# A hybrid convolution and state-space block with a ternary FFN on one core: out-projection bias by one-row matmuls, two loads exchanged, and the first FFN step's instruction lists reordered

## What is computed

```
x1 = LN(x)                                  # no weights
u, v = split(x1 @ W_in + b_in)              # 512 -> 2 x 512
v = silu(v); v = conv3(v, conv_w) + conv_b  # depthwise, along the 8192 tokens
h_t = a * h_(t-1) + b * v_t ;  y_t = c * h_t + d * v_t     # a = sigmoid(logit_a)
out = (u * silu(y)) @ W_out + b_out         # b_out is the bias of this change
x = x + LN( LN_weighted(out + x1) )
f = gelu(LN(x) @ ternary(W1).T + b1)        # 512 -> 2048
x = x + LN( f @ ternary(W2).T + b2 )        # 2048 -> 512
```

## Time and profile before

| | |
|---|---|
| median of 3 runs | 1426.45 us (1423.77 to 1429.59) |
| the profiled execution | 1427.28 us |
| its span, first to last instruction | 1425.1 us |
| mean granted TensorE clock | 0.998 |
| TensorE matmul (PE), weight load (PEld) | 98%, 45% of the span |
| VectorE, ScalarE, GpSimd | 79%, 62%, 29% |
| HBM read, written | 31.49 MB, 16.78 MB |

### The profile page before, as it was taken

How to read it: one execution, slowest core, us unless ns; L and a number is a source line. 1 busy time by engine, 2 the same in 40 slices (tenths; PEclk the granted TensorE clock), 3 DMA queues, 4 the chain that set the end, 5 groups by cost and what they waited for, 6 DMA issues and landing times.

```text
span 1425.1 us, 19037 instructions
## 1 busy us (share of the span) xinstructions
PE 1402.7 (98%) x6528; PEld 642.0 (45%) x6528; DVE 1119.9 (79%) x1892; ACT 878.4 (62%) x1263; POOL 418.3 (29%) x518
## 2 busy tenths in 40 slices
PE   7999999999999999999999999999999999999997
PEld 5444444444444444444444444444444444444443
DVE  7999987867878687796867878677796877998734
ACT  7899575646656565665656756466565656753443
POOL 4234151321413233142321413224132321523221
PEclk9999999999999999999999999999999999999999
DMA  9712321311312112111311203123121231001200
GB/s 249 242 43 77 72 71 19 89 30 30 89 19 72 30 45 75 30 60 31 82 37 30 75 15 89 31 30 89 24 66 30 51 69 30 30 1 30 59 31 30
DMA packets 155985, 82.00 MB, mean 58 GB/s; under 512 B 132721, under 2 KB 132721, under 8 KB 155761
## 3 DMA queue, kind: packets, MB, share of 16 engines
q1 hardware_dynamic: 155888, 80.79, 22.2%
HBM read 31.49 MB, written 16.78 MB: 34 GB/s over the span
## 4 chain that ended last, share of the span: by engine, by line
PE 82%; DVE 6%; issue 3%; ACT 1%; POOL 1%; DMA 0%; SPq 0%; DVEq 0%; ACTq 0%; POOLq 0%
PE f2b L580 14%; PE f2b L581 14%; PE f1b L551 13%; PE f1b L552 13%; PE misc L519 6%; PE misc L517 6%; PE misc L518 6%; PE misc L533 3%; PE misc L531 3%; PE misc L532 3%; DVE bn L775 1%; POOL rsc L2009 0%; DVE vl L851 0%; DVE g_lo L895 0%; DVE ring L793 0%
## 5 line engine op out<-in xcount | busy, mean ns | idle before, releaser
L580 PE MATMUL f2b<-w,ring 128*128 128x512 fp8e5 x1008 | 382.2, 379 | 1.2 <-DVE ring L793 1.0
L581 PE MATMUL f2b<-w,ring 128*128 128x512 fp8e5 x1008 | 382.0, 379 | 0.0
L551 PE MATMUL f1b<-x3T,w 128*128 128x512 f16 x960 | 364.0, 379 | 0.6 <-DMA x3T<-tp 0.4
L552 PE MATMUL f1b<-x3T,w 128*128 128x512 f16 x960 | 363.8, 379 | 0.0
L1587 ACT ACTIVATE ring<-f1b,par 128x512 f32<-128x512 f32 x256 | 175.1, 684 | 232.9 <-PE f1b L552 232.6
L2008 POOL TENSOR_SCALAR ve<-mv 128x4 f32<-128x4 f32 (+2 forms) x88 | 35.5, 403 | 731.0 <-DVE mv L785 730.8
L793 DVE SCALAR_TENSOR_TENSOR ring<-ring,f_sc 128x512 f16<-128x512 f32 x256 | 210.1, 835 | 40.8 <-ACT ring L1597 40.6
L1597 ACT ACTIVATE ring<-ring,f_sc 128x512 f16<-128x512 f32 x256 | 180.1, 710 | 0.0
L517 PE MATMUL misc<-x1T,win_hi 128*128 128x512 f16 x456 | 172.9, 379 | 0.0
L518 PE MATMUL misc<-x1T,win_hi 128*128 128x512 f16 x456 | 172.9, 379 | 0.0
L519 PE MATMUL misc<-x1T,win_lo 128*128 128x512 f16 x456 | 172.9, 379 | 0.0
(11 more groups left out here) (219 smaller groups left out, 2017.2 us busy)
## 6 DMA issues: line engine op xcount, KB each, us to landing
out_dram<-hb SPq DMA_DIRECT2D x64, 256.0 KB, 2.0
xs<-x_dram SPq DMA_DIRECT2D x14, 1024.0 KB, 5.6
ring<-w1t_dram SPq DMA_DIRECT2D x3, 1024.0 KB, 12.3
stage<-w2t_dram SPq DMA_DIRECT2D x3, 1024.0 KB, 8.5
x1T<-tp SPq DMA_TRANSPOSE x68, 3.1
...
```

Of the source, the lines that this page charges most:

```text
L551: pe.matmul(b[:, :], w, src[:, k, :], start=k == 0, stop=False)
L552: mm = pe.matmul(b[:, :], w, src[:, KC + k, :], start=False, stop=k == KC - 1)
L580: pe.matmul(f2b[q][:, :], h_hi[:, i % H_SLOTS, qs], w2[:, j, :], start=j == 0, stop=False)
L581: mm = pe.matmul(f2b[q][:, :], h_lo[:, i % H_SLOTS, qs], w2[:, j, :], start=False, stop=j == FC - 1)
```

## The change

1. **Bias.** VectorE's four `add_bias(j)` of tile 0 go. `wo_forward` (VectorE) computes one column o_fwd, the product of both scales; `out_bias` on ScalarE writes b_out times o_fwd into one row of xn (fp32), and `out_bias` on TensorE multiplies a row of ones (1 x 128) with it (1 x 512) into each of the four accumulators of o(0, j) with start=True; the matmuls of o(0, j) then add to them. `h_add(0, j)` waits for x1_hi instead of ob_ok.
2. **Loads.** SP issues the third x tile ahead of W_out.
3. **Warming.** `keep_warm` issues 4 warm matmuls behind each of the first three transposes of tile 0, 12 in place of 30; `ffn_scale` (TensorE) goes from the list's first place to behind it, `setup_params` (VectorE) from the first place to behind x_stats(1, 3).
4. **Lists.** The hand-written lists of all engines up to the end of the first FFN step are put in another order, with new ORDER and SIGNED. Among it: centre_tap(1, 0) and (1, 1) go from ahead of the transposes of x3 to behind the copies of x3; o(1, 1) and o(1, 2) get f2(0, 4) between them, o(1, 2) and o(1, 3) f2(0, 5); in_proj("v", 3, 0) to (3, 3) come ahead of f1(0, 12). The loops of later steps are unchanged.

The diff, cut to its core (VectorE's and ScalarE's lists behind o(0, j) are left out for the most part):

```diff
 
 
 W1_CHUNK, W2_CHUNK = "w1", "w2"
-ORDER = [(W1_CHUNK, 0), (W1_CHUNK, 2), (W1_CHUNK, 3), (W1_CHUNK, 1), (W1_CHUNK, 5), (W1_CHUNK, 6), (W1_CHUNK, 10), (W1_CHUNK, 9),
-         (W2_CHUNK, 0), (W1_CHUNK, 7), (W1_CHUNK, 4), (W1_CHUNK, 8), (W2_CHUNK, 1), (W1_CHUNK, 11), (W2_CHUNK, 2), (W2_CHUNK, 3),
-         (W2_CHUNK, 4), (W2_CHUNK, 7), (W2_CHUNK, 5), (W2_CHUNK, 6), (W2_CHUNK, 8), (W1_CHUNK, 14), (W1_CHUNK, 13), (W1_CHUNK, 15),
-         (W1_CHUNK, 12), (W2_CHUNK, 11), (W2_CHUNK, 9), (W2_CHUNK, 10), (W2_CHUNK, 13), (W2_CHUNK, 12), (W2_CHUNK, 14), (W2_CHUNK, 15)]
-SIGNED = (1, 1, 1, 1, 2, 2, 3, 3, 4, 2, 2, 3, 5, 3, 8, 6, 7, 7, 7, 7, 9, 10, 10, 10, 10, 9, 9, 9, 11, 11, 11, 11)
+ORDER = [(W1_CHUNK, 0), (W1_CHUNK, 3), (W1_CHUNK, 2), (W1_CHUNK, 1), (W1_CHUNK, 6), (W1_CHUNK, 5), (W1_CHUNK, 4), (W1_CHUNK, 7),
+         (W1_CHUNK, 9), (W1_CHUNK, 11), (W1_CHUNK, 8), (W1_CHUNK, 10), (W2_CHUNK, 0), (W2_CHUNK, 1), (W2_CHUNK, 2), (W2_CHUNK, 3),
+         (W2_CHUNK, 4), (W2_CHUNK, 5), (W2_CHUNK, 7), (W2_CHUNK, 9), (W2_CHUNK, 6), (W2_CHUNK, 11), (W2_CHUNK, 10), (W2_CHUNK, 8),
+         (W1_CHUNK, 14), (W1_CHUNK, 15), (W1_CHUNK, 12), (W1_CHUNK, 13), (W2_CHUNK, 12), (W2_CHUNK, 13), (W2_CHUNK, 14), (W2_CHUNK, 15)]
+SIGNED = (1, 1, 1, 1, 2, 2, 2, 2, 3, 3, 3, 3, 4, 5, 6, 7, 8, 8, 8, 9, 8, 9, 9, 9, 10, 10, 10, 10, 11, 11, 11, 11)
 
 
...
             transposes("t1", 1)
+            load_x(2)
             sp.dma_start(wo_raw, w_out_d).then_inc(wout_in, 16)
-            load_x(2)
             load_w1(0)
             load_w1(1)
...
 
-                out_ = take("o", c, j)
+                out_ = take("o", c, j) if c > 0 else bank("o", 0, j)
                 js = slice(j * P, (j + 1) * P)
                 if c == 0 and j == 0:
                     pe.wait_ge(wo_l, KC)
                 for k in range(KC):
                     pe.wait_ge(glo_ok, KC * c + k + 1)
-                    pe.matmul(out_[:, :], g_hi[:, k, js], wo_hi[:, k, :], start=k == 0, stop=False)
+                    pe.matmul(out_[:, :], g_hi[:, k, js], wo_hi[:, k, :], start=c > 0 and k == 0, stop=False)
                     pe.matmul(out_[:, :], g_hi[:, k, js], wo_lo[:, k, :], start=False, stop=False)
                     mm = pe.matmul(out_[:, :], g_lo[:, k, js], wo_hi[:, k, :], start=False, stop=k == KC - 1)
...
             def keep_warm():
 
-                pe.wait_ge(x1_lo, 3)
-                warm(14)
-                for k in (1, 3):
-                    pe.wait_ge(win_l, k)
-                    warm(8)
+                for j in range(NB - 1):
+                    wait_transposed(pe, block_no["t1", 0, j])
+                    warm(4)
 
             def transpose_x3(n):
...
+            def out_bias():
+
+                pe.wait_ge(ob_ok, 2)
+                for j in range(NB):
+                    pe.matmul(take("o", 0, j)[:, :], ones[0:1, :], xn[0:1, :], start=True, stop=False)
+
...
             pe.wait_ge(const_ok, 2)
-            ffn_scale()
             pe.wait_ge(x1_hi, 1)
             warm(6)
             win_sum(1)
             warm(6)
             keep_warm()
+            ffn_scale()
             in_proj("v", 0, 0, v_mm)
             in_proj("v", 0, 1, v_mm)
...
             in_proj("v", 1, 2, v_mm)
-            wo_sum()
             in_proj("v", 1, 3, v_mm)
             in_proj("u", 0, 0, u_mm)
+            wo_sum()
             in_proj("u", 0, 1, u_mm)
             in_proj("u", 0, 2, u_mm)
             in_proj("u", 0, 3, u_mm)
+            out_bias()
             o(0, 0)
             o(0, 1)
             o(0, 2)
...
             f1(0, 5)
             f1(0, 6)
             f1(0, 7)
+            f2(0, 0)
+            f1(0, 8)
             f2(0, 1)
-            f1(0, 8)
+            f1(0, 9)
             f2(0, 2)
-            f1(0, 9)
+            f1(0, 10)
             f2(0, 3)
-            f1(0, 10)
-            f2(0, 4)
             o(1, 0)
             o(1, 1)
+            f2(0, 4)
             o(1, 2)
+            f2(0, 5)
             o(1, 3)
-            f2(0, 5)
+            f2(0, 6)
             f1(0, 11)
-            f2(0, 6)
+            f2(0, 7)
+            in_proj("v", 3, 0, v_mm)
+            f2(0, 8)
+            in_proj("v", 3, 1, v_mm)
+            in_proj("v", 3, 2, v_mm)
+            in_proj("v", 3, 3, v_mm)
+            f2(0, 9)
             f1(0, 12)
-            f2(0, 7)
+            f2(0, 10)
             f1(0, 13)
-            f2(0, 8)
             f1(0, 14)
-            in_proj("v", 3, 0, v_mm)
-            in_proj("v", 3, 1, v_mm)
-            f2(0, 9)
-            in_proj("v", 3, 2, v_mm)
-            f2(0, 10)
+            f2(0, 11)
             f1(0, 15)
-            f2(0, 11)
...
                 else:
-                    ve_.wait_ge(ob_ok, j + 1)
+                    ve_.wait_ge(x1_hi, j + 1)
                     ve_.wait_ge(wo_sc_ok, 2)
                 dst = hb_of(c)[:, j, :]
...
 
+            def wo_forward():
+
+                after("wo inverse")
+                ve_.wait_ge(scale_ok, 3)
+                ve_.tensor_scalar(o_fwd[:, :], wq[:, 5:6], w_mul[:, 0:1], ACT_SCALE / 2.0 ** 14, ALU.mult, ALU.mult).then_inc(ob_ok, 1)
...
@@ -1194,118 +1199,116 @@
             t_lo("t1", 0, 0)
             win_square(1)
             t_lo("t1", 0, 1)
+            x_stats(1, 0)
+            x_stats(1, 1)
             win_total(1)
-            x_stats(1, 0)
+            aggr(0, 1, 0)
             win_power(1)
-            x_stats(1, 1)
+            aggr(0, 1, 1)
             win_bound(1)
-            aggr(0, 1, 0)
-            aggr(0, 1, 1)
+            t_lo("t1", 0, 2)
             win_scale(1)
-            t_lo("t1", 0, 2)
             x_stats(1, 2)
             t_lo("t1", 0, 3)
+            aggr(0, 1, 2)
             x_stats(1, 3)
-            aggr(0, 1, 2)
+            setup_params()
+            aggr(0, 1, 3)
             setup_split(0)
-            aggr(0, 1, 3)
             setup_split(1)
             setup_split(2)
             setup_split(3)
+            v_scale()
+            ffn_total()
             t_lo("t1", 1, 0)
-            v_scale()
             t_lo("t1", 1, 1)
             win_max_u(0)
             t_lo("t1", 1, 2)
             win_max_u(1)
+            ffn_exponent()
+            win_square(0)
             t_lo("t1", 1, 3)
-            win_square(0)
-            taps(0, 0, True)
             win_total(0)
             win_power(0)
             win_bound(0)
             win_scale(0)
-            ffn_total()
+            ffn_inverse()
+            taps(0, 0, True)
+            setup_split(KC + 0)
             taps(0, 1, True)
-            setup_split(KC + 0)
             setup_split(KC + 1)
-            ffn_exponent()
-            ffn_inverse()
             ffn_scale()
             setup_split(KC + 2)
+            u_bias()
...
+            y(0, 0)
+            y(0, 1)
+            wo_norm()
+            scan(0, 2)
+            taps(0, 3, False)
+            wo_total()
+            y(0, 2)
+            wo_power()
             aggr(0, 2, 1)
-            wo_norm()
             aggr(0, 2, 2)
+            wo_bound()
+            gate_scale()
             aggr(0, 2, 3)
-            scan(0, 0)
-            taps(0, 1, False)
-            wo_total()
-            y(0, 0)
-            wo_power()
-            taps(0, 2, False)
-            wo_bound()
-            scan(0, 1)
             wo_inverse()
-            scan(0, 2)
-            y(0, 1)
-            taps(0, 3, False)
-            wo_scale()
             ve_.wait_ge(par_ok, 5)
             gate(0, 0)
-            y(0, 2)
+            wo_scale()
+            scan(0, 3)
+            gate(0, 1)
+            y(0, 3)
             setup_out_proj(0)
-            scan(0, 3)
             ve_.wait_ge(g_sc_ok, 1)
             gate_lo(0, 0)
-            y(0, 3)
-            gate(0, 1)
+            wo_forward()
             gate(0, 2)
+            gate_lo(0, 1)
             setup_out_proj(1)
-            setup_out_proj(2)
-            gate_lo(0, 1)
             gate(0, 3)
             gate_lo(0, 2)
+            setup_out_proj(2)
             setup_out_proj(3)
...
+            taps(1, 0, False)
+            ternary(8)
+            ternary(9)
+            taps(1, 1, True)
+            ternary(10)
+            taps(1, 2, True)
             taps(1, 1, False)
-            threshold(1)
+            ternary(11)
+            ternary(12)
+            scan(1, 0)
+            taps(1, 3, True)
             taps(1, 2, False)
-            ternary(6)
-            ternary(7)
-            ternary(8)
-            taps(1, 3, True)
-            ternary(9)
-            ternary(10)
-            ternary(11)
             lo(0, 0)
+            y(1, 0)
+            ternary(13)
+            scan(1, 1)
             lo(0, 1)
             taps(1, 3, False)
-            scan(1, 0)
-            scan(1, 1)
-            y(1, 0)
-            ternary(12)
+            y(1, 1)
+            lo(0, 2)
             scan(1, 2)
             scan(1, 3)
-            ternary(13)
-            lo(0, 2)
-            y(1, 1)
             y(1, 2)
```

(93 more changed lines are left out.)

207 lines of the change are left out of this document (92 added, 115 removed).

## The result

The changed kernel takes 1428.12 us (median of 20 runs, 1424.50 to 1432.93), the kernel before 1425.24 (20 runs beside them, 1423.77 to 1429.59). The ratio is 1.0023, interval 1.0015 to 1.0031: **2.9 us slower** in the medians, 3.3 by the ratio, where 3.2 us faster was forecast. The profiled execution has a span of 1427.0 us against 1425.1. Of the 20 runs of the changed kernel 6 stand apart, at 1431.8 to 1432.9 us with a mean granted clock of 0.995; the others take 1424.5 to 1429.2 us at 0.997 to 0.999, and the profiled one is of these.

The account below looks back on a forecast made before the run. TensorE was taken as the bound, with VectorE's list and data arrival bounding the start. Earlier o(0,0) -0.8, clock -1.7 and reordered lists -0.7 gave -3.2 us, from 1426.45 to 1423.2; range 1418.0 to 1427.5.

Parts of the forecast that it names:

- Part 1: At the start, the new warming lets v(0,0) begin 3.2 us earlier, of which 1.9 us are left at the scale.
- The wait for wm_sq: Ahead of win_sum(0), TensorE arrives at 24.3 us and waits 0.9 us for win_square(0).
- Part 2: VectorE's list up to o(0,0): o(0,0) can start at 55.5 to 55.7 us instead of 56.48, 0.8 us earlier.
- the forecast waits for centre_tap(0,3) and for the edge: Two new VectorE waits ahead of o(0,0): about 0.4 us for ScalarE's centre tap, 1.1 to 1.5 us for GpSimd's edge copy.
- Part 3: Bias matmuls ahead of o(0,0), 0.85 us each, fill idle time at about no cost; o(0,3) ends 2.5 us earlier.
- term of -1.7 us: Behind o(0,0)'s start: the bias matmuls keep TensorE from idling, so the drop to 1.2 GHz goes, -1.7 us.
- a case with this price: At the bias matmuls: if one row takes next to nothing, TensorE idles 3.5 us and the slow clock stays, sum -1.5.
- Part 4: Reordered lists from x3's transposes to 138 us: -0.7 us, bounds +2 and -2.3.
- 0 to 0.8 us late: At v(3,0), four groups earlier than before: its last transpose can come 0 to 0.8 us late.
- rival C: W1's reload in flight slows tile 3's transposes; TensorE idles 3 us ahead of v(3,0), clock falls: +3.0, 1429.5 us; chance 0.12.
- Behind 170 us the order is the same: After the first FFN step, from 170 us on: the order of work is unchanged, so no gain or loss was counted.

Follow-up runs that it names:

- experiment 7: The kernel before with the new keep_warm alone, and ffn_scale behind it on TensorE: 1428.02 us, ratio 1.0007.
- experiment 6: The fixed kernel with W_out loaded ahead of the third x tile again: 1429.66 us, ratio 1.0016.
- experiment 4: The fixed kernel with tile 0's bias added by VectorE again, without the one-row matmuls: 1425.76 us, ratio 0.9998.
- 9: The changed kernel with the bias matmuls over all 128 rows: 1426.88 us, ratio 1.0005.
- 11: The fixed kernel with the bias added by VectorE and 14 warm matmuls ahead of o(0,0): 1423.82 us, ratio 0.9986.
- Experiment 1: The changed kernel with W1's reload issued behind tile 3's four transposes instead of ahead of them: 1427.03 us, ratio 1.0001.
- experiment 2: The changed kernel with f1(0,15) ahead of f2(0,11) on TensorE instead of behind it: 1426.34 us, ratio 1.0010.
- the fixed kernel: The changed kernel with W1's reload behind tile 3's transposes and f1(0,15) ahead of f2(0,11): 1424.83 us, ratio 0.9994.
- experiment 10: The changed kernel measured and profiled again, with no further edit, against the kernel before: 1428.37 us, ratio 1.0019.

## Why the prediction was wrong

**Part 1 held.** v(0,0) came 3.06 us earlier for 3.2, 1.99 us of it were left at the scale for 1.9, and experiment 7 shows that without the lists and loads none is left at o(0,0). The wait for wm_sq (0.9 us, as forecast) takes part of the rest.

**Part 2 held.** o(0,0) at 55.46 for 55.5 to 55.7. The exchange of the loads was sized well on the changed side (x came in time but for 0.6 us, and the forecast waits for centre_tap(0,3) and for the edge didn't come) and too small on the other: undoing it costs 3.1 us by the ratios (experiment 6), because the wait for x is 3.6 us long once all ahead of it is earlier, and the clock stays low for longer.

**Part 3 failed in its term of -1.7 us.** Its duration, 0.85 us each, was near (3.63 us for four, 0.91 each), its place and its cover were right. Wrong was "with them the array is not idle, so the clock drop should go". With one row the drop is gone in one execution out of six that were profiled; with 128 rows in all four. The first profile of the changed kernel happened to be the one, so it seemed to bear the step out; only further profiles showed otherwise. In its place: no gain clear of noise from the one-row biases (experiment 4), and 1.7 to 2.0 us less where the clock held, by full rows (9) or by warm matmuls (11). The prediction had a case with this price, -1.5 instead of -3.2, but tied it to the matmuls taking next to nothing; they took their full time and the clock fell all the same.

**Part 4 failed at v(3,0).** Its -0.7 us were met and passed ahead of that (-3.76 + 2.65 = -1.1 us behind o(0,3)), with the wait for h_add(1,0) gone and f2's waits of 0.4 us as walked. But the "0 to 0.8 us late" of the last transpose was 2.8 us, and 1.5 us of slow clock came behind it. I had named this as rival C with its price (3.0 + 1.7 us) and gave it 0.12. The forecast used the landing time of undisturbed transposes, though the earlier trace rows had 6.2 us beside loads and SP's list has the reload directly ahead. It knew that chunk (w2,6) releases the reload, but not when: at 127.4 in the profile, 0.65 us ahead of the first transpose. Experiment 1 confirms the cause, 3.1 us by the ratios. The size in the first profile was partly chance: three further profiles wait 1.4 to 1.9 us, with no slow clock behind.

**"Behind 170 us the order is the same" overlooked what is ahead of 170.** f1(0,15) and v(3,3) had changed places, which took the cover of x3T's transposes from 11.2 to 6.9 us. SP waits for f1(0,15) before it overwrites x3T, and from there the transposes need 7.3 us. It cost 1.9 us in the first profile, 1.1 of them by slow landings, and 0.6 in the second; experiment 2 puts it at 1.8 us by the ratios, barely clear of noise. No term or rival had it.

**The sum again.** Against the kernel before, by ratios: the fixed kernel, with both waits short or gone, -0.9 us; the two waits together +4.1; the changed kernel +3.3, and +2.7 in experiment 10. My -3.2 without the clock's 1.7 is -1.5, which the fixed kernel's interval (-2.1 to +0.6) takes in. The range left C out although its price was worked out. Its +3.0 is close to the result, but in part by luck: its 1.5 us for f1(0,12) and its chunks didn't come (there is no such wait), and the wait for x3T, which it didn't have, stood in their place.
